# Two edits in a two-layer model on one core: a projection's bias written into its PSUM banks by ScalarE instead of added by TensorE, and the order of transposes and logits in the dispatch

## The reference

```
# layer 0, MLP: a soft mixture with 8 experts of 128 slots
logits   = einsum('bsd,etd->bset', xn, se)
dispatch = softmax(logits, axis=1)               # over the tokens
slots    = einsum('bsd,bset->betd', xn, dispatch)
h        = gelu(slots @ w1) @ w2                  # then combined back
# layer 1, mixer: a Mamba-2 scan
zxbcdt = u @ W_in + b_in                          # z 512, xs 512, B 64, C 64, dt 8
dt     = softplus(zxbcdt[..., 1152:] + dt_bias)
h = exp(dt*A) * h + dt*xs * B ;  y = h . C        # over 2048 tokens
y = (y + D_skip*xs) * silu(z) ;  out = y @ W_out + b_out
```

## Time and profile before

| | |
|---|---|
| median of 3 runs | 1705.84 us |
| the profiled execution | 1705.65 us, of which the trace spans 1703.9 us |
| TensorE busy | 1613.9 us (95% of the span) |
| VectorE busy | 1218.9 us (72%) |
| ScalarE busy | 747.7 us (44%) |
| GpSimd busy | 541.8 us (32%) |

### The profile page before, as it was taken

How to read it: one execution, slowest core, us unless ns; L and a number is a source line. 1 busy time by engine, 2 the same in 40 slices (tenths; PEclk the granted TensorE clock), 3 DMA queues, 4 the chain that set the end, 5 groups by cost and what they waited for, 6 DMA issues and landing times. The chain is left out here.

```text
span 1703.9 us, 25741 instructions
## 1 busy us (share of the span) xinstructions
PE 1613.9 (95%) x9344; PEld 1379.7 (81%) x9344; DVE 1218.9 (72%) x2687; ACT 747.7 (44%) x1467; POOL 541.8 (32%) x443
## 2 busy tenths in 40 slices
PE   7899989989999999999989999999889999999996
PEld 5688878878888888867877888888778788889896
DVE  6777688764467756646888999999867936676663
ACT  3333333443357234427236666666421314454442
POOL 2100020000000003322535666666400024777764
PEclk9999999999999999999989999999999999999999
DMA  7000000010010000201024222222241125566553
GB/s 228 5 1 2 1 1 1 1 50 1 1 50 26 11 3 19 90 32 69 27 79 174 84 77 78 78 78 78 65 156 50 50 64 166 137 159 154 139 124 37
DMA packets 80392, 112.60 MB, mean 66 GB/s; under 512 B 15998, under 2 KB 60170, under 8 KB 79884
## 3 DMA queue, kind: packets, MB, share of 16 engines
q1 hardware_dynamic: 66316, 92.48, 16.9%
q0 software_dynamic: 12288, 17.31, 5.6%
q10 hardware_dynamic: 1664, 1.18, 0.2%
HBM read 82.64 MB, written 27.68 MB: 65 GB/s over the span
## 5 line engine op out<-in xcount | busy, mean ns | idle before, releaser
L3099 POOL DMA_INDIRECT out<-k_eo,idx x64 | 117.0, 1828 | 74.6 <-DVE k_eo L3195 57.3
L1988 POOL DMA_INDIRECT k_xe<-rows_dram,idx x64 | 82.4, 1287 | 178.9 <-DVE idx L3032 140.6
L1819 PE MATMUL d_pO<-d_sp,d_raw 128*128 128x257 f32 x512 | 116.1, 385 | 1.9 <-DVE x L1239 1.7
L1819 PEld LDWEIGHTS d_pO<-d_sp,d_raw 128*128 128x128 f32 x512 | 96.9, 192 | 16.4 <-DVE x L1239 2.4
L545 ACT ACTIVATE b_p<-b_pS,b_nmax 128x384 f32<-128x384 f32 (+16 forms) x32 | 38.1, 1190 | 131.8 <-DVE b_nmax L686 131.8
L61 PE MATMUL b_pO<-b_vh,b_ph 128*128 128x256 f32 x302 | 87.9, 291 | 7.0 <-DVE b_pl L668 6.8
L63 PE MATMUL b_pO<-b_vl,b_ph 128*128 128x256 f32 x302 | 85.4, 283 | 0.0
L62 PE MATMUL b_pO<-b_vh,b_pl 128*128 128x256 f32 x302 | 85.4, 283 | 0.0
L2181 ACT ACTIVATE g_dlm<-d_cumb,mod 128x128 f32<-128x128 f32 x256 | 78.4, 393 | 3.4 <-DMA d_cumb<-cum_dram 3.4
L339 POOL TENSOR_TENSOR x<-x,b_vrow 128x256 f32<-128x256 f32 x32 | 24.1, 785 | 169.6 <-DVE b_hs L614 169.5
L3154 ACT ACTIVATE k_act_g<-k_pg 128x512 f32<-128x512 f32 x64 | 38.3, 598 | 87.3 <-PE k_pu L63 73.5
(11 more groups left out here) (575 smaller groups left out, 5377.6 us busy)
## 6 DMA issues: line engine op xcount, KB each, us to landing
d_cumb<-cum_dram SPq DMA_DIRECT2D x32, 512.0 KB, 4.2
k_wf<-in_WgT SPq DMA_DIRECT2D x16, 512.0 KB
k_wf<-in_WuT SPq DMA_DIRECT2D x16, 512.0 KB
k_wf<-in_WdT SPq DMA_DIRECT2D x16, 512.0 KB
rows_dram<-h_hx SPq DMA_DIRECT2D x32, 136.0 KB, 3.8
x<-in_x SPq DMA_DIRECT2D x8, 512.0 KB, 9.6
d_w<-in_w SPq DMA_DIRECT2D x4, 1024.0 KB, 6.2
uT_dram<-d_ug SPq DMA_DIRECT2D x16, 256.0 KB, 2.4
```

What stands on the lines that cost most here:

```text
L1819: last = nc.tensor.matmul(pO[:, t % 2, 0:PW], raw[e][:, t * P:(t + 1) * P], proc[e], start=e == 0, stop=e == E - 1)
L1988: nc.gpsimd.indirect_dma_start(out=m.xe[:, e % 2, t, :], out_offset=None, in_=m.rows, in_offset=bass.IndirectOffsetOnAxis(ap=column(m, e, ...
L3099: nc.gpsimd.indirect_dma_start(out=out, out_offset=bass.IndirectOffsetOnAxis(ap=column(m, e, t), axis=0), in_=eo[:, e % 2, t, :], in_offse ...
```

## The change

In the scan, ScalarE copies the bias of xs and z (1024 values, loaded once into all partitions as `wide_bias`) into the banks `px` and `pz` after their last readers, and the projection adds onto them: 12 matmuls, none of them with start, where there were 12 and one more in each bank for the bias. `pbc` keeps its bias matmul. TensorE waits for these copies (`px_set`, `pz_set`) where it waited for the readers. In the dispatch, TensorE and ScalarE take the first group's transposes and copy ahead of the last logits group.

The adding helper and the place of the bias in SBUF (over `bb`'s first columns, read for the last time by job 0's projection):

```diff
+def exact_onto(nc, out, ah, al, bh, bl, stop):
+
+
+    nc.tensor.matmul(out, ah, bh, start=False, stop=False, skip_group_check=True)
+    nc.tensor.matmul(out, al, bh, start=False, stop=False, skip_group_check=True)
+    return nc.tensor.matmul(out, ah, bl, start=False, stop=stop, skip_group_check=True)
...
+        m.wide_bias = placed("wide_bias", [P, ZX], kept + 24 * KB)
```

The dispatch, ScalarE and then TensorE:

```diff
                     if et + 1 < E:
-                        for g in range(0 if et else 1, NG):
+                        for g in range(0 if et else 1, NG - 1):
                             keep(b, et + 1, g)
-                    for g in range(2):
-                        copy_t(b, et, g)
+                    copy_t(b, et, 0)
+                    if et + 1 < E:
+                        keep(b, et + 1, NG - 1)
+                    copy_t(b, et, 1)
...
                     if et + 1 < E:
-                        logits(b, et + 1)
+                        logits(b, et + 1, range(NG - 1))
                         if b and et >= 2:
                             state_steps(0, et - 2)
                     pe.wait_ge(s["exp_done"], b * E + et + 1)
+                    transposes(b, ("exp", et, 0))
+                    if et + 1 < E:
+                        logits(b, et + 1, range(NG - 1, NG))
                     if b * E + et >= 2:
                         pe.wait_ge(s["sl_scaled"], b * E + et - 1)
                     if b and et < 2:
                         pe.wait_ge(s["x_done"], b * NTB)
-                    transposes(b, ("exp", et, 0))
```

The scan: SyncE's first DMA, ScalarE in `evacuate`, its new step and where it is called, TensorE in `project`:

```diff
+            sp.dma_start(m.wide_bias[:], w["b_in"][0:ZX].partition_broadcast(P)).then_inc(s["bias_in"], 16)
             sp.dma_start(neg[:], w["A_log"].partition_broadcast(P)).then_inc(s["a_in"], 16)
...
                 nc.scalar.activation(zr[:, b], pz[:], ACT.Tanh, scale=0.5).then_inc(s["th_done"], 1)
+                if is_job(n + 1):
+                    act.wait_ge(s["bias_in"], 16)
+                    act.wait_ge(s["xs_copied"], n + 1)
+                    nc.scalar.copy(px[:], m.wide_bias[:, INNER:ZX]).then_inc(s["px_set"], 1)
+
+            def gate_bias(n):
+                act.wait_ge(s["zr_done"], n)
+                nc.scalar.copy(pz[:], m.wide_bias[:, 0:INNER]).then_inc(s["pz_set"], 1)
...
             decay(0)
+            gate_bias(1)
             late_exp()
...
                 if is_job(n + 1):
                     decay(n + 1)
+                if is_job(n + 2):
+                    gate_bias(n + 2)
...
-                for dst, o, width, freed in ((pbc, ZX, 2 * STATE, "bc_copied"), (px, INNER, INNER, "xs_copied"), (pz, 0, INNER, "zr_done")):
+                for dst, o, width, freed in ((pbc, ZX, 2 * STATE, "bc_copied"), (px, INNER, INNER, "px_set"), (pz, 0, INNER, "pz_set")):
                     pe.wait_ge(s[freed], n)
...
                     for k in range(CH):
-                        exact_matmul(nc, dst[:, 0:width], uh[:, b, k, :], ul[:, b, k, :], winh[:, k, o:o + width],
-                                     winl[:, k, o:o + width], k == 0, False)
-                    last = nc.tensor.matmul(dst[:, 0:width], onesr[:], bb[:, o:o + width], start=False, stop=True)
+                        ah, al, bh, bl = uh[:, b, k, :], ul[:, b, k, :], winh[:, k, o:o + width], winl[:, k, o:o + width]
+                        if freed == "bc_copied":
+                            exact_matmul(nc, dst[:, 0:width], ah, al, bh, bl, k == 0, False)
+                        else:
+                            last = exact_onto(nc, dst[:, 0:width], ah, al, bh, bl, k == CH - 1)
+                    if freed == "bc_copied":
+                        nc.tensor.matmul(dst[:, 0:width], onesr[:], bb[:, o:o + width], start=False, stop=True)
```

More of the change, by code:

```diff
@@ L1734, in logits_of, with logits @@
                 return last
-            def logits(b, et):
-                for g in range(NG):
+            def logits(b, et, groups):
+                for g in groups:
                     pe.wait_ge(s["raw_done"], bank(b, et - 1, g))
@@ L2026, in state_space @@
         staged = lambda n: (n + 1) // B * 48
-        names = ("loaded split_high split_low gain0 first_ready first_gelu base shifts bits groups same below0 below1 below ip_ready bc_copied xs_copied th_done bt_ready bt_copied g_ready gm_done "
+        names = ("loaded bias_in px_set pz_set split_high split_low gain0 first_ready first_gelu base shifts bits groups same below0 below1 below ip_ready bc_copied xs_copied th_done bt_ready bt_copied g_ready gm_done "
                  "zr_done zeroed dd_done le_done m_done dtx_done xw_done xD_done i_ready st_ready y_ready "
@@ L2518, in project @@
                         pe.wait_ge(s["f_kept"], 1)
-                    if n == 1 and freed == "xs_copied":
+                    if n == 1 and freed == "px_set":
                         correlate(0)
                     for k in range(CH):
-                        exact_matmul(nc, dst[:, 0:width], uh[:, b, k, :], ul[:, b, k, :], winh[:, k, o:o + width],
-                                     winl[:, k, o:o + width], k == 0, False)
-                    last = nc.tensor.matmul(dst[:, 0:width], onesr[:], bb[:, o:o + width], start=False, stop=True)
+                        ah, al, bh, bl = uh[:, b, k, :], ul[:, b, k, :], winh[:, k, o:o + width], winl[:, k, o:o + width]
[5 more added lines that the diff above has]
+                        nc.tensor.matmul(dst[:, 0:width], onesr[:], bb[:, o:o + width], start=False, stop=True)
                 last.then_inc(s["ip_ready"], 1)
```

## The result

| | before | after |
|---|---|---|
| median | 1707.62 us (6 runs, 1704.69 to 1709.07) | 1696.92 us (6 runs, 1694.81 to 1699.56) |
| span of the profiled execution | 1703.9 us | 1695.4 us |
| TensorE busy | 1613.9 us | 1603.5 us |
| ScalarE busy | 747.7 us | 778.6 us |

The account below looks back on a forecast made before the run. TensorE's own work was taken to set the scan's pace. Terms -13.3 + 3.2 + 3.0 - 2.5 = -9.6 us took the profiled 1705.65 to 1696.1, predicted median 1696.2, range 1689.5 to 1702.0.

Parts of the forecast that it names:

- matmuls, jobs 3 to 31: Scan: two bias matmuls of 0.23 us fewer per job, 29 x 0.46 = 13.3 us gained if TensorE stays the pace-setter.
- late jobs: Scan, four jobs near 1177 us: `within` waits longer for the exponential, 0.9, 0.9, 0.9 and 0.5, together 3.2 us lost.
- start of the scan: Scan's start: ScalarE's copies wait for the bias to land, delaying job 1's z; 3.0 us lost, ends 2.0 and 5.0.
- dispatch: Slot tiles: waits for ScalarE's copy of the transposes go, less additional switches and first-tile waiting; 2.5 us gained.
- The reckoning of its spare time: Scan: VectorE's waits for router logits, 1.26 us per two jobs, against 0.92 lost; 0.34 left, so VectorE doesn't take over.
- The px copy: ScalarE, ahead of the router's exponential: copy takes 0.48 us, leaving 0.07 us in an even job, 0.44 in an odd one.
- rival 4: Scan: `within` waits for the exponential in every job, ScalarE sets the pace; slower, 1711 us, chance 0.05.
- The upper end of 6 us: Late jobs' loss if the px copy takes 0.1 us more and the even jobs wait as well.
- It moves along: Scan's start: TensorE's 0.79 us wait for GpSimd shifts with the projection, taking only job 2's 0.46 us with it.
- From 4.0 us: Dispatch: the waits of the slots' first product, less about 0.2 for the second batch's eighth, give 3.8 us gained.
- The second: Rival, scan: ScalarE's lateness never reaches `within` and the start costs 2 us; 1691.1 us, chance 0.25.
- The third: Rival, scan: px copy takes 0.2 us more, even and late jobs wait; 1701.0, or 1703.5 without dispatch gain; chance 0.20.

Follow-up runs that it names:

- the run with the copy behind: Changed kernel with ScalarE's copy of the bias into px behind the router's exponential instead of ahead of it: 1692.53 us, 0.9918 against before.
- job 1 by TensorE: Changed kernel with job 1's bias by TensorE as before and the wide bias loaded by ScalarE after job 1's projection: 1692.49 us, 0.991 against before.
- px twice: Changed kernel with the copy into px made twice, TensorE waiting for the second: 1706.75 us, 0.9992 against before.
- jobs 1 and 2 by TensorE: Both job 1's bias by TensorE and px copy behind the exponential, extended to job 2's bias by TensorE, load behind its projection: 1694.99 us.
- that with the copies ahead: Jobs 1 and 2's bias by TensorE, with job 3's px and pz copies ahead of job 2's decay instead of behind it: 1692.05 us.
- both edits alone: Kernel before with only the scan's edit: 1701.24 us, 0.9964; and with only the dispatch's edit: 1701.2 us, 0.9962.
- both cures: Changed kernel with job 1's bias by TensorE and the px copy behind the router's exponential: 1688.02 us, on another chip 1692.12 us.
- the two with the wait filled: Unread matmuls ahead of the wait near 540 us: in the changed kernel (also in its last jobs) 1696.41 us; with jobs 1 and 2's bias by TensorE 1696.1.

## Why the prediction was right or wrong

**The sum was right by errors that cancelled.** 1696.2 forecast, 1696.9 measured. Luck has a part in how close that is. The forecast took 9.6 us from an execution of 1705.65, and six runs put the kernel before at 1707.62. By the medians of six runs the change gave 10.7 us, by the spans of the two profiled executions 8.5. Term by term, in the profiled execution:

| term | forecast | measured |
|---|---|---|
| matmuls, jobs 3 to 31 | -13.3 | -13.3 (20.94 to 20.02 per pair) |
| late jobs | +3.2 | +2.9 |
| start of the scan | +3.0 | +4.8, of which 3.2 behind job 1's projection |
| dispatch | -2.5 | -6.8 |
| clock near 540 and 1226 us | none | +1.5 and +1.3 |
| the beginning, not the change's | none | +0.75 |

The start's 4.8 is the 3.41 of the table of shifts and the 3 x 0.46 that jobs 3 to 5 had gained by then (the last bias matmul ahead of 936.74 us, at 936.51, is job 5's). The terms sum to -8.8, the spans differ by 8.5; no row names the 0.3 between them.

**Matmuls**: right. The distance between starts, not the 0.40 of the duration, was the price.

**VectorE**: right in what counted, 0.34 us of lateness per even job (up to 0.37 forecast). The reckoning of its spare time was not: 0.34 us per pair of jobs was to be left, and 0.77 is, because two instructions of each even job got 0.97 us shorter in sum. The forecast held VectorE's own work constant; the error went to the safe side by luck.

**The px copy**: forecast 0.48 us of ScalarE's queue, measured 0.52 (it lasts 0.61), and 0.08 us left in the even job, 0.07 forecast. The estimate from the Trainium skill, ScalarE: Activation LUTs, What ACT_TABLE_LOAD costs, was 0.52; by that rule, the trace agrees. The doubled copy tested the slack: my rival 4 priced x us above 0.48 at x - 0.07 and x - 0.44 in alternate jobs. For the two copies' 1.18 us (x = 0.70) that is 0.63 and 0.26, 12.9 us over 29 jobs; measured were 0.30 us per job in the steady ones and 9.8 in all. Even and odd jobs wait alike there, 0.23 and 0.24 us: VectorE's lateness goes once TensorE waits, which my rule left out.

**Late jobs**: right in mechanism and size, 0.97 us in the worst against 0.9. The run with the copy behind splits it into 0.53 for the copy and 0.44 for VectorE. Two of the four are milder than forecast, 0.39 and 0.30 us against 0.9 and 0.5, and that two early jobs wait too (0.1 us each) wasn't foreseen. The upper end of 6 us doesn't come out of the forecast's own rates: 0.1 us more per copy gives 3.2 + 0.4 for the late jobs and 13 x 0.03 = 0.4 for the even ones, 4.0.

**The start**: the mechanism and the 3.2 us behind job 1 were right (3.0 forecast). They came about as 2.26 us of lateness, where the forecast had 2.8 less 0.25, and 0.9 of low clock, which it had left open. The landing was 3.55 us, 3.8 forecast. The Trainium skill, DMA: Bandwidth & Descriptors, Anatomy of one DMA, states its fit for DMAs that GpSimd issues; the estimate of 3.2 us took it over for SyncE's, and the measurement lies between. "It moves along" was wrong: low clock from 909 to 913 us cost more on top, 1.5 us by the comparison with the scan's edit alone, whose trace has the same work in the same order, the same 20.5 us of low clock before, none from 909 to 913, and lost only 1.9 us up to 936.74 where the changed kernel lost 3.4.

**The dispatch**: the step that failed is the price of a wait. "From 4.0 us" took the idle time in the bracket for the whole cost. The 0.16 us in which TensorE's last matmul still ran come on top, 0.44 us a tile instead of 0.29; and "0.07 us a tile, an estimate" for the additional change was nothing. 14 x 0.44 = 6.2; the tiles came 0.48 to 0.54 us closer together, and the last 0.04 to 0.1 has no row that names it. The new waiting for the first exponential was forecast at 0.15 us per batch; in the first batch 7 x 0.51 = 3.6 against the 3.44 of the shift leaves 0.1.

**The stages behind**: the forecast said that what the scan wins reaches the end undiminished. The work's gain did; the last jobs took 1.3 us back by the clock, which the profile of before couldn't show, since its clock didn't fall there. Between the instructions that stand at 1209 and 1245 us before, the seven traces with low clock in these jobs lost 1.3 to 2.5 us, and the five others that have them unfilled lost nothing.

**The rivals.** The second (ScalarE's lateness never reaches `within`) fell by the earlier trace rows's successor. The third's 0.2 us more for the copy were 0.04. The fourth's mechanism, a wait for the exponential in every job, was reached by doubling the copy, its 1711 us were not.

## What to carry to other kernels

A wait on TensorE costs the distance from the start of the last matmul ahead to the start of the next, less what one takes at full pace; the idle time in a bracket leaves the last one's drain out (0.44 us against 0.29 here). When work moves to an engine that is half idle, look for its place in that engine's queue, not its share: 0.52 us ahead of the exponential cost 2 us in 29 jobs, the same copy behind it nothing, and a copy behind a DMA wait made TensorE wait 4.4 us for data that, by the run with the copy ahead of it, had landed some 5 us earlier. Where a change is worth some us, compare shifts place by place, and read the granted clock of each place before giving a difference to the change.

## What the runs showed of the hardware

TensorE's clock falls behind a wait in one trace and not behind the identical wait in another. At the wait of 2.03 us near 540 us, the same in every kernel here, it fell in 6 of the 12 traces in which the wait stands as it is (the changed kernel twice, job 1 by TensorE, px twice, jobs 1 and 2 by TensorE, and that with the copies ahead) and stayed full in 6 (the kernel before, both edits alone, px behind, both cures twice); in the two with the wait filled it stayed full. Each of the six falls shifted what follows by 1.45 to 1.48 us, read between 534 and 553 us. In the scan's last jobs the clock fell in the changed kernel and not in the kernel before; near 1400 us it fell in all but the px copy behind and the first run of both cures.

The traces show an order in it. In each of the 14 the stretches of low clock start on the marks of one even raster, and that raster lies differently against the program from trace to trace. Sorted by how far the end of the wait near 540 us lies behind the last mark, the six traces that kept the clock stand together, at 0.21 to 0.70 us, and so do the six that lost it, from 1.9 us on to 0.14 us behind the next mark. In two of them the wait ended at 538.80 and 538.81 us (jobs 1 and 2 by TensorE; both cures, the second time), with the raster 0.2 us apart, and the clock fell in the first alone. The places near 730, 1245 and 1400 us part the 14 traces in the same way; the last jobs, whose waits differ between the kernels, don't. The Trainium skill, TensorE: Matmul & The Clock Gate, Part 1: The HAM clock gate, says that the circuit that watches TensorE runs freely and isn't started with the kernel, so that where a transition falls varies from run to run; these traces agree. The two kernels with the wait filled stood at about 2.1 and 2.6 us, among those that fell, and kept the clock: together this makes it likely that the wait is needed for the fall, and that filling it prevented one. No run sets the place of the raster, so this is read from the traces and not tested by a change.

ScalarE writes a PSUM bank of 512 fp32 columns from SBUF in 0.58 to 0.62 us, as fast as it reads one out (0.59). A load of 512 KB, broadcast to all partitions, landed 3.55 us behind its DMA at the head of the stage and 6.6 us behind it among the stage's other loads.
